# A selective scan on one core: eight turned states instead of seven, and delta's bias inside TensorE's product

## Chip, cores, metric

One core of a Trainium2 chip runs the whole program. The metric is the device time in microseconds (us) of one execution.

## What is computed

Two layers over eight images of 192 channels and 48 x 48 points: a selective state space layer and an attention layer. The scan of the first layer carries the time, and the change lies in it:

```python
dts = einsum('bkrl,kdr->bkdl', dts, dt_w)              # 12 rows -> 384 channels
delta = softplus(dts + dt_b[None, :, :, None])
A = -exp(A_logs)                                       # K = 4 directions, 384 channels, 16 states
def step(h, xs_t):
    d_t, u_t, B_t, C_t = xs_t
    h = h * exp(d_t[..., None] * A) + (d_t * u_t)[..., None] * B_t[:, :, None, :]
    y = einsum('bkdn,bkn->bkd', h, C_t)                # sum over the 16 states of C times h
    return (h, y)
```

All of it is float32. softplus(x) is computed as max(x, 0) + ln(1 + exp(-|x|)).

## The kernel before

The eight images are a loop (`Fori`). Each has a `front` (depthwise convolution, gelu, the projection to B, C and delta's 12 rows), a `scan_phase`, a `back` (layer norm, gate, output projection) and `attention`. The scan phase goes through K = 4 directions k of NC = 6 chunks each, so 24 **chunks** of CH = 384 positions an image, and 192 in all. Directions 1 and 3 run over the image by columns, so that their y is read and written with strides.

In each chunk a loop goes over the 16 **states** i, and in each state over J = 3 tiles j of 128 channels. The engines share one state after the other, each with an instruction order of its own that is written out by hand and never changes at run time; semaphores hold them together. Below, **slot i** is the part of an engine's loop with that i.

- ScalarE (ACT), slot i: three exponentials E(i, j) = exp(delta x A) into PSUM banks 2 to 4 (L1406). E(i, j) may start once VectorE has finished scan(i-1, j), which reads the same bank. Between and behind these three stand the other jobs: turned products P (L1365), `hold_state` (L1341), copies of a row of C into PSUM bank 1 (`c_copy`, L1357), the steps of softplus for the next chunk (x L1294, abs L1297, exp L1300, ln L1309), the stores of the last chunk's y (L1389, in slots 2 and 3) and the copies of two projection tiles (`unit_out`, only for k < 3).
- VectorE (DVE), slot i: three scans (L1098), one for each j. Scan(i, j) needs E(i, j).
- The product with C and the sum over the states have three ways. POOL_N: GpSimd multiplies (L1634), TensorE adds with a product by the identity (`state_sum`, L698). DVE_N: VectorE multiplies one slot later (`times_c`, L1120; needs the copied row), TensorE adds the same way. TURN_N: TensorE turns a 128 x 128 block so that positions lie on partitions (`turn`, T, L676, bank 0), ScalarE multiplies by C's column while it copies (P), and TensorE turns it back into the sum (`turned_sum`, S, L685). A state has three such blocks, numbered through the chunk: T(n), P(n), S(n) with n = 0 to 20. There is one bank for turned blocks, so T(n) waits for P(n-1) and P(n) for T(n): the two engines take turns.
- TensorE (PE), slot m: `slot` issues the turns, turned sums and state sums of tables TURN_AT and SUM_AT. Ahead of them come `delta_tile` (L664, delta's product for the next chunk into bank 1, in slots 1, 4, 7) and `unit` (L724, the projection tiles, bank 1, in slots 10 and 14), and behind them an addition of the previous y (L747, L750).
- GpSimd (POOL): delta x u x B of each state (L1624), at most three states ahead of the scans, the three C products (L1634), and delta x u once a chunk (L1613).

Bank 1 is shared in time by the C rows, delta's product and the projection tiles. ScalarE's and TensorE's queues are in order: what waits holds up all that stands behind it.

## Time and profile before

| | |
|---|---|
| median of 3 runs | 14456.84 us (14454.49 to 14457.94) |
| the profiled execution | 14456.79 us, its span 14455.0 us |
| scan phases in it | 8, each 24 chunks; the first from 161.58 us to about 1438 us |
| busy share of the span (page) | VectorE 87%, TensorE 84%, ScalarE 83%, GpSimd 69% |

A row of the timeline gives start, duration, engine, line, operation, and in brackets how long the engine was idle before it and who ended the wait. Durations of neighbours on one engine overlap a little, so the text goes from start to start.

### The profile page before, as it was taken

How to read it: one execution, taken by the hardware profiler on the slowest of the kernel's cores; microseconds unless marked ns; L12 is line 12 of the kernel's file. 1: busy time of each engine (PE TensorE's matmuls, PEld its weight loads, DVE VectorE, ACT ScalarE, POOL GpSimd, SP SyncE). 2: the span in 40 equal slices, each digit the busy share in tenths (PEclk: the TensorE clock that was granted, in tenths of full speed). 3: DMA queues.
4: the chain of work that ended last, by engine and by line, in shares of the span. 5: the costliest groups of instructions: out<-in, count | busy, mean ns of one | idle time of the engine just before them, and what ended most of it. 6: DMA issues, size and time to landing. Idle time of an engine off the chain costs nothing.

```text
span 14455.0 us, 270626 instructions
## 1 busy us (share of the span) xinstructions
PE 12184.4 (84%) x71128; PEld 7313.9 (51%) x71128; DVE 12643.8 (87%) x13653; ACT 11957.6 (83%) x25498; POOL 10046.1 (69%) x4006
## 2 busy tenths in 40 slices
PE   6887988879888798888988879888898888988889
PEld 4554554545555455554555545555455554555545
DVE  8999679997799977999689996899959999599995
ACT  5888788887888878887888878888788886888868
POOL 5999069990699807998079970899708996099960
PEclk9999999999999999999999999999999999999999
DMA  3443124440344303443034430344204442044420
GB/s 115 133 132 123 29 94 131 132 126 22 99 132 132 120 22 107 133 141 102 22 114 130 141 97 22 119 132 142 89 22 126 132 139 84 22 133 130 140 79 27
DMA packets 908103, 1470.10 MB, mean 102 GB/s; under 512 B 38913, under 2 KB 891905, under 8 KB 893665
## 3 DMA queue, kind: packets, MB, share of 16 engines
q1 hardware_dynamic: 906560, 1452.37, 31.5%
q8 instruction: 623, 10.21, 0.3%
q14 instruction: 920, 7.53, 0.2%
HBM read 1350.07 MB, written 102.17 MB: 100 GB/s over the span
## 4 chain that ended last, share of the span: by engine, by line
issue 39%; POOL 22%; PE 22%; DVE 10%; ACT 5%; DVEq 1%; ACTq 1%; POOLq 0%; DMA 0%; SPq 0%
POOL area L1624 18%; DVE area L1098 7%; PE ps L934 4%; PE ps L915 4%; PE ps L698 3%; POOL area L1613 2%; POOL area L1634 2%; PE ps L804 1%; ACT ps L1406 1%; DVE area L1120 1%; PE ps L676 1%; PE ps L780 1%; ACT area L1365 1%; DVE area L356 1%; PE ps L685 1%
## 5 line engine op out<-in xcount | busy, mean ns | idle before, releaser
L1098 DVE TENSOR_TENSOR_SCAN area<-ps,hst,area 128x384 f32<-128x384 f32 x9216 | 8566.2, 995 | 59.6 <-ACT ps L1406 46.9
L1624 POOL TENSOR_TENSOR area<-area 128x1152 f32<-128x1152 f32 x3072 | 7993.9, 2637 | 45.6 <-POOL area L1613 45.6
L1406 ACT ACTIVATE ps<-area,a_neg 128x384 f32<-128x384 f32 x9216 | 5171.5, 580 | 820.1 <-DVE area L1098 801.5
L698 PE MATMUL ps<-area,ident 128*128 128x384 f32 x10368 | 3845.6, 503 | 375.0 <-POOL area L1634 185.3
L676 PE MATMUL ps<-ident,area 128*128 128x128 f32 x12096 | 2117.6, 284 | 1353.7 <-ACT area L1365 1348.8
L698 PEld LDWEIGHTS ps<-area,ident 128*128 128x128 f32 x10368 | 1878.7, 195 | 1835.0 <-ACT area L1389 414.8
L676 PEld LDWEIGHTS ps<-ident,area 128*128 128x128 f32 x12096 | 1391.3, 141 | 2619.8 <-ACT area L1365 2019.7
L1365 ACT ACTIVATE area<-ps,area 128x384 f32<-128x384 f32 x4032 | 2304.7, 572 | 462.1 <-PE ps L676 438.6
L1567 ACT ACTIVATE area<-ps,t_neg,area 128x384 f32<-128x384 f32 x3456 | 2126.1, 667 | 113.6 <-PE ps L915 24.5
L1608 POOL TENSOR_TENSOR area<-area,ones 128x2304 f32<-128x2304 f32 x8 | 43.5, 5443 | 3060.6 <-ACT area L1321 2939.0
L685 PE MATMUL ps<-ident,area 128*128 128x128 f32 x12096 | 2017.1, 276 | 134.0 <-ACT area L1365 133.7
L1634 POOL TENSOR_TENSOR area<-area 128x1152 f32<-128x1152 f32 x576 | 1515.6, 2631 | 191.1 <-ACT hst L1341 190.5
L685 PEld LDWEIGHTS ps<-ident,area 128*128 128x128 f32 x12096 | 1459.8, 142 | 300.6 <-ACT area L1365 195.2
L1120 DVE TENSOR_TENSOR area<-area,ps 128x1152 f32<-128x1152 f32 x1152 | 1532.9, 1331 | 35.7 <-ACT ps L1357 35.7
L934 PE MATMUL ps<-area 64*64 64x384 f32 x13824 | 1479.5, 486 | 40.8 <-ACT area L1515 32.6
L915 PE MATMUL ps<-area 64*64 64x384 f32 x13824 | 1486.9, 489 | 12.7 <-ACT area L1491 12.7
L934 PEld LDWEIGHTS ps<-area 64*64 64x64 f32 x13824 | 614.1, 134 | 572.8 <-issue 159.1
L915 PEld LDWEIGHTS ps<-area 64*64 64x64 f32 x13824 | 627.2, 135 | 514.6 <-issue 85.1
L1188 DVE TENSOR_TENSOR area<-area 128x1920 f32<-128x1920 f32 (+1 forms) x32 | 43.4, 1356 | 874.0 <-ACT area L1515 874.0
L356 DVE SCALAR_TENSOR_TENSOR area<-area,w_dw 128x1152 f32<-128x1152 f32 (+1 forms) x640 | 802.8, 1331 | 0.0
L1357 ACT ACTIVATE ps<-area 128x384 f32<-128x384 f32 x1152 | 562.5, 488 | 24.2 <-DVE area L1120 8.3
L1613 POOL TENSOR_TENSOR area<-area 128x1152 f32<-128x1152 f32 x192 | 505.6, 2634 | 109.5 <-DVE area L1045 109.5
(140 smaller groups left out, 10052.8 us busy)
## 6 DMA issues: line engine op xcount, KB each, us to landing
area<-bc_rows SPq DMA_DIRECT2D x1536, 768.0 KB, 6.7
xz<-x_normed SPq DMA_DIRECT2D x144, 288.0 KB, 3.5
area<-in_x SPq DMA_DIRECT2D x18, 1728.0 KB, 10.0
area<-x_padded SPq DMA_DIRECT2D x24, 1250.0 KB, 5.6
z_raw<-z_st SPq DMA_DIRECT2D x144, 192.0 KB, 2.6
area<-z_raw SPq DMA_DIRECT2D x8, 3456.0 KB, 12.3
x_padded<-x_st SPq DMA_DIRECT2D x120, 200.0 KB, 7.3
x_normed<-area SPq DMA_DIRECT2D x9, 1728.0 KB, 7.9
```

Source lines behind the costliest of these rows:

```text
L676: i = e.matmul(ps[:, 0, j * 128:(j + 1) * 128], hb[:, n % NH, j, tt * 128:(tt + 1) * 128], ident[:], is_transpose=True)
L685: i = e.matmul(ps[:, 5 + j, tt * 128:(tt + 1) * 128], ht[:, tt, j * 128:(j + 1) * 128], ident[:], start=False, stop=False, is_transpose=True)
L698: m = e.matmul(ps[:, 5 + j, 0:CH], ident[:], hb[:, i % NH, j], start=i == 0, stop=i == N - 1)
L915: i = e.matmul(ps[64 * g:64 * g + 64, (2 * n + h) % 6, 0:CH], kz[64 * h:64 * h + 64, p, m * 128 + 64 * g:m * 128 + 64 * g + 64], q_v[64 * ...
L934: i = e.matmul(ps[64 * h:64 * h + 64, 6 + r, 0:CH], vt[64 * r:64 * r + 64, p, m, 64 * h:64 * h + 64], pb[64 * r:64 * r + 64, (2 * n + h) % ...
L1098: e.tensor_tensor_scan(rev(hb[:, i % NH, j], k), rev(ps[:, 2 + j, 0:CH], k), rev(dbu[:, i % NH, j], k), hst[:, i, j:j + 1], ALU.mult, ALU. ...
L1120: e.tensor_tensor(hb[:, i % NH], hb[:, i % NH], ps[:, 1:2, 0:CH].broadcast_to([128, J, CH]), ALU.mult).then_inc(hcs, 1)
L1365: e.activation(ht[:, tt], ps[:, 0, 0:CH], ACT.Copy, scale=c_t[:, ds(t + (k % 2 * MT + tt), 1), k // 2 * N + n]).then_inc(turn_cp, 1)
L1406: e.activation(ps[:, 2 + j, 0:CH], dlt[:, par, j], ACT.Exp, scale=a_neg[:, j, k, i:i + 1]).then_inc(da, 1)
L1567: e.activation(pb[:, w % 8], ps[:, w % 6, 0:CH], ACT.Exp, scale=ksc[:, p, 2 * m + h:2 * m + h + 1], bias=t_neg[:, 2 * p + h:2 * p + h + 1] ...
L1624: e.tensor_tensor(dbu[:, i % NH], du[:, par], row_b[:, q % 2, i % ROWS:i % ROWS + 1].broadcast_to([128, J, CH]), ALU.mult).then_inc(dbus, 1)
L1634: e.tensor_tensor(hb[:, i % NH], hb[:, i % NH], row_c[:, q % 2, i % ROWS:i % ROWS + 1].broadcast_to([128, J, CH]), ALU.mult).then_inc(hcp, 1)
```

## The change

One more state is turned (8 of 16), VectorE keeps five products (2, 5, 8, 12, 15), GpSimd its three. The blocks are n = 0 to 23, and the last two, 22 and 23, are done in slots 0 and 1 of the next chunk (TURN_AT[16]).

Delta's bias is a thirteenth row of `w_dt`, and the matching row of `dts` is one, so that TensorE adds it. The step x of softplus is gone: abs reads bank 1, ln writes into `du` instead of bank 1, and VectorE's delta step reads max(x, 0) from bank 1. The softplus steps start two slots earlier for each tile (abs in slots 1, 4, 7 at the slot's end, where it waits for `dp_mm`; exp and ln in the two slots after, behind E(i, 0)), and VectorE's delta step stands behind scan(i, 0) of slots 3, 6, 9. On TensorE `delta_tile` and `unit` move behind the slot's first turn and the previous turned sum (`between`).

```diff
-TURN_N = (1, 3, 6, 7, 10, 12, 13)
-TURN_AT = {2: (0,), 3: (1, 2), 4: (3, 4), 5: (5,), 7: (6, 7), 8: (8, 9), 9: (10, 11), 11: (12, 13), 12: (14,),
-           13: (15, 16), 14: (17, 18), 15: (19, 20)}
+TURN_N = (1, 3, 6, 7, 10, 11, 13, 14)
+TURN_AT = {2: (0,), 3: (1, 2), 4: (3, 4), 5: (5,), 7: (6, 7), 8: (8, 9), 9: (10, 11), 11: (12, 13), 12: (14, 15),
+           13: (16, 17), 14: (18, 19), 15: (20, 21), 16: (22, 23)}
-SUM_AT = {0: 3, 2: 4, 4: 6, 5: 7, 8: 10, 9: 12, 11: 13, 14: 16, 15: 17}
+SUM_AT = {0: 3, 2: 4, 4: 6, 5: 7, 8: 10, 9: 12, 12: 14, 15: 17}
-X_AT = {2: 0, 5: 1, 8: 2}
-SOFT = ((3, "abs", 0), (4, "exp", 0), (5, "ln", 0), (6, "abs", 1), (7, "exp", 1), (8, "ln", 1),
-        (9, "abs", 2), (10, "exp", 2), (11, "ln", 2))
+SOFT = ((1, "abs", 0), (2, "exp", 0), (3, "ln", 0), (4, "abs", 1), (5, "exp", 1), (6, "ln", 1),
+        (7, "abs", 2), (8, "exp", 2), (9, "ln", 2))
+STEP_AT = {3: 0, 6: 1, 9: 2}
@@ sync: after the loads of the constants
+            e.wait_ge(consts, 16 * len(loads))
+            for k in range(K):
+                e.dma_start(w_dt[DT0[k] + R:DT0[k] + R + 1, k].rearrange("o (j p) -> o j p", j=J),
+                            t["b_dt"][:, :, k:k + 1].rearrange("p j o -> o j p"),
+                            allow_slow_non_contiguous=True).then_inc(bias_row, 16)
@@ tensor
+            e.wait_ge(bias_row, 16 * K)
...
-                def slot(g, m):
+                def slot(g, m, between=None):
...
                         turned_sum(g, before[-1])
+                    if between:
+                        between()
...
-                        if m < 2 and last:
-                            slot(g - 1, N + m)
...
+                        if m < 2 and last:
+                            slot(g - 1, N + m, between)
+                            slot(g, m)
+                        else:
+                            slot(g, m, between)
@@ vector
-                e.scalar_tensor_tensor(out=dlt[:, par, j], in0=dlt[:, par, j], scalar=0.0, in1=ps[:, bank, 0:CH],
+                e.scalar_tensor_tensor(out=dlt[:, par, j], in0=ps[:, bank, 0:CH], scalar=0.0, in1=du[:, par, j],
...
+                            if nxt and j == 0 and i in STEP_AT:
+                                delta(g + 1, 1 - par, STEP_AT[i])
@@ scalar
-                if op == "x":
+                if op == "abs":
                     e.wait_ge(dp_mm, g * 3 + (j + 1))
-                    e.activation(x, ps[:, bank, 0:CH], ACT.Identity, bias=b_dt[:, j, k:k + 1]).then_inc(dp_rd, 1)
+                    e.activation(y, ps[:, bank, 0:CH], ACT.Abs).then_inc(dp_a, 1)
...
-                    e.activation(ps[:, bank, 0:CH], y, ACT.Ln, bias=1.0).then_inc(dp_a, 1)
+                    e.activation(y, y, ACT.Ln, bias=1.0).then_inc(dp_a, 1)
...
-                             ACT.Copy).then_inc(xp_ev, 1)
+                             ACT.Identity, bias=dt_one[64:128]).then_inc(xp_ev, 1)
...
-                    if nxt and i in (5, 8, 11):
-                        e.wait_ge(dp_v, g * 3 + (3 + (i - 2) // 3))
+                    if nxt and i in (2, 5, 8):
+                        e.wait_ge(dp_v, g * 3 + (3 + (i - 2) // 3 + 1))
...
+                            if nxt and j == 0:
+                                for at, op, d in SOFT:
+                                    if at == i and op != "abs" and (last or d):
+                                        softplus(g + 1, 1 - par, op, d)
...
-                            elif last:
-                                turned_products(g - 1, *last, N - 1, j)
+                            if i < 2 and last:
+                                turned_products(g - 1, *last, N - 1 + i, j)
```

**ScalarE, end of slot 4 and start of slot 5.** Before (L1365 is P(2), L1341 the hold, L1300 softplus's exp of tile 0, L1406 E(5, 0)):

```order
L1365 ACTIVATE area<-ps,area 128x384 [waits turn_sum]
L1341 ACTIVATE hst<-area 128x3
L1299 ISA
L1300 ACTIVATE area<-area 128x384 [waits dp_a]
L1405 REGISTER_ALU
L1406 ACTIVATE ps<-area,a_neg 128x384 [waits scan]
```

After (L1368 is P(2), L1308 the abs of tile 1, L1409 E(5, 0), L1311 softplus's exp of tile 1, then P(3)):

```order
L1368 ACTIVATE area<-ps,area 128x384 [waits turn_sum]
L1344 ACTIVATE hst<-area 128x3
L1307 REGISTER_ALU
L1308 ACTIVATE area<-ps 128x384 [waits dp_mm]
L1408 REGISTER_ALU
L1409 ACTIVATE ps<-area,a_neg 128x384 [waits scan]
L1310 REGISTER_ALU
L1311 ACTIVATE area<-area 128x384 [waits dp_a]
```

A step that read ScalarE's own result stood there; now one stands there that waits for TensorE's product of this same slot.

**ScalarE, slot 13.** Before: E(13, 0), E(13, 1), P(14), E(13, 2):

```order
L1406 ACTIVATE ps<-area,a_neg 128x384 [waits scan]
L1405 REGISTER_ALU
L1406 ACTIVATE ps<-area,a_neg 128x384 [waits scan]
L1363 REGISTER_ALU
L1365 ACTIVATE area<-ps,area 128x384 [waits turn_sum,turn_mm]
L1405 REGISTER_ALU
L1406 ACTIVATE ps<-area,a_neg 128x384 [waits scan]
```

After: E(13, 0), P(14), E(13, 1), E(13, 2), P(15):

```order
L1409 ACTIVATE ps<-area,a_neg 128x384 [waits scan]
L1366 REGISTER_ALU
L1368 ACTIVATE area<-ps,area 128x384 [waits turn_sum,turn_mm]
L1408 REGISTER_ALU
L1409 ACTIVATE ps<-area,a_neg 128x384 [waits scan]
L1408 REGISTER_ALU
L1409 ACTIVATE ps<-area,a_neg 128x384 [waits scan]
L1366 REGISTER_ALU
L1368 ACTIVATE area<-ps,area 128x384 [waits turn_sum,turn_mm]
```

P(14) has moved ahead of E(13, 1).

**TensorE, slot 14.** Before: the unit (L724), T(17), S(16), then T(18) and S(17):

```order
L724 MATMUL ps<-xz,w_in 128x384 [waits xz_in,hcs]
L724 MATMUL ps<-xz,w_in 128x384
L674 REGISTER_ALU
L676 MATMUL ps<-ident,area 128x128 [waits turn_cp]
L676 MATMUL ps<-ident,area 128x128 x2
L685 MATMUL ps<-ident,area 128x128 [waits turn_cp]
L685 MATMUL ps<-ident,area 128x128 x2
```

After: T(18) (L682), S(17) (L691), the unit (L732), the sum of state 12 (L704), T(19):

```order
L682 MATMUL ps<-ident,area 128x128 [waits turn_cp]
L682 MATMUL ps<-ident,area 128x128 x2
L691 MATMUL ps<-ident,area 128x128 [waits turn_cp]
L691 MATMUL ps<-ident,area 128x128 x2
L728 REGISTER_ALU
L732 MATMUL ps<-xz,w_in 128x384 [waits xz_in,hcs]
L732 MATMUL ps<-xz,w_in 128x384
L704 MATMUL ps<-area,ident 128x384 [waits hcs]
L704 MATMUL ps<-area,ident 128x384 x2
L680 REGISTER_ALU
L682 MATMUL ps<-ident,area 128x128 [waits turn_cp]
L682 MATMUL ps<-ident,area 128x128 x2
```

Both the unit and a state sum now stand between the two turns of the slot.

## Rows read from the trace of the kernel before

**Rows 1.** Busy time by window: length, PE, PEld, DVE, ACT, POOL, clock, DMA, GB/s.

```profile
905.00:1380.00 475.00, 378.45 (x1761) 232.81 (x1760) 473.91 (x513) 416.94 (x963) 467.24 (x181) 1.00 0.42 134
```

**Rows 2.** Groups by line: VectorE's scans; busy, mean ns, idle before and releasers.

```profile
L1098 DVE TENSOR_TENSOR_SCAN area<-ps,hst,area 128x384 f32<-128x384 f32 x9216 | 8566.2, 995 | 59.6 <-ACT ps L1406 46.9 <-POOL area L1624 5.5 <-PE ps L698 3.8
```

**Rows 3.** Timeline of VectorE: scans, one C product, delta step, scans.

```profile
1021.18 8.28 DVE L1098 TENSOR_TENSOR_SCAN area<-ps,hst,area 128x384 f32<-128x384 f32 x9
1029.38 1.33 DVE L1120 TENSOR_TENSOR area<-area,ps 128x1152 f32<-128x1152 f32 x1
1030.62 5.55 DVE L1098 TENSOR_TENSOR_SCAN area<-ps,hst,area 128x384 f32<-128x384 f32 x6
1036.09 0.53 DVE L1045 SCALAR_TENSOR_TENSOR area<-area,ps 128x384 f32<-128x384 f32 x1
1036.54 2.83 DVE L1098 TENSOR_TENSOR_SCAN area<-ps,hst,area 128x384 f32<-128x384 f32 x3
```

**Rows 4.** Timeline of GpSimd over one chunk.

```profile
1064.54 10.40 POOL L1624 TENSOR_TENSOR area<-area 128x1152 f32<-128x1152 f32 x4 [0.24 <-POOL area L1613]
1074.89 2.64 POOL L1634 TENSOR_TENSOR area<-area 128x1152 f32<-128x1152 f32 x1
1077.48 10.42 POOL L1624 TENSOR_TENSOR area<-area 128x1152 f32<-128x1152 f32 x4
...
1114.53 2.62 POOL L1613 TENSOR_TENSOR area<-area 128x1152 f32<-128x1152 f32 x1
1117.39 10.40 POOL L1624 TENSOR_TENSOR area<-area 128x1152 f32<-128x1152 f32 x4 [0.24 <-POOL area L1613]
```

**Rows 5.** One line, L1613 (once a chunk), first image: duration min/median/max, first and last start.

```profile
L1613 POOL TENSOR_TENSOR area<-area x24: 2615/2637/2674, 155.9 to 1378.6; 128x1152 f32<-128x1152 f32 x24
```

**Rows 6.** Timeline of ScalarE and TensorE, slots 11 to 13, direction 2.

```profile
1001.96 0.57 ACT L1406 ACTIVATE ps<-area,a_neg 128x384 f32<-128x384 f32 x1
1002.47 0.56 ACT L1365 ACTIVATE area<-ps,area 128x384 f32<-128x384 f32 x1
...
1003.08 0.55 PE L676 MATMUL ps<-ident,area 128*128 128x128 f32 x3 [1.16 <-ACT area L1365]
...
1003.46 0.49 PE L685 MATMUL ps<-ident,area 128*128 128x128 f32 x3
...
1004.44 2.10 PE L698 MATMUL ps<-area,ident 128*128 128x384 f32 x6
...
1006.37 0.49 PE L676 MATMUL ps<-ident,area 128*128 128x128 f32 x3
...
1006.90 0.58 ACT L1365 ACTIVATE area<-ps,area 128x384 f32<-128x384 f32 x1 [0.91 <-PE ps L676]
```

**Rows 7.** Timeline of all three, slots 12 to 15, direction 1.

```profile
628.29 0.56 ACT L1365 ACTIVATE area<-ps,area 128x384 f32<-128x384 f32 x1
...
633.37 0.58 ACT L1365 ACTIVATE area<-ps,area 128x384 f32<-128x384 f32 x1 [1.54 <-PE ps L676]
...
637.31 1.46 PE L724 MATMUL ps<-xz,w_in 96*128 96x384 f32 x4
...
638.60 0.49 PE L676 MATMUL ps<-ident,area 128*128 128x128 f32 x3
...
639.13 0.58 ACT L1365 ACTIVATE area<-ps,area 128x384 f32<-128x384 f32 x1 [0.80 <-PE ps L676]
639.61 1.08 ACT L1406 ACTIVATE ps<-area,a_neg 128x384 f32<-128x384 f32 x2
...
640.22 1.93 DVE L1098 TENSOR_TENSOR_SCAN area<-ps,hst,area 128x384 f32<-128x384 f32 x2 [0.49 <-ACT ps L1406]
```

**Rows 8.** Timeline: delta's product on TensorE and the step that reads it.

```profile
381.97 0.81 PE L664 MATMUL ps<-area,w_dt 128*128 128x384 f32 x2
...
382.82 0.58 ACT L1294 ACTIVATE area<-ps,b_dt 128x384 f32<-128x384 f32 x1 [0.38 <-PE ps L664]
```

**Rows 9.** One line, L1389, the stores of y: duration min/median/max.

```profile
L1389 ACT ACTIVATE area<-ps x576: 464/644/860, 225.6 to 13970.7; 128x384 f32<-128x384 f32 x192
```

More of the change, by code:

```diff
@@ L216, in build @@
         prepared = sem("prepared")
+        bias_row = sem("bias_row")
         exp_a = sem("exp_a")
@@ L731, in body, with between @@
                     for m in range(N):
-                        j = DELTA_AT.get(m) if nxt else None
-                        if j is not None:
-                            e.wait_ge(hcs, gd + (1, 2, 3)[j])
-                            delta_tile(*nxt, j, 1)
-                        if k < UK and m in UNIT_AT:
-                            unit(k, h, gd, UNIT_AT.index(m))
-                        if m < 2 and last:
-                            slot(g - 1, N + m)
+                        def between():
+                            j = DELTA_AT.get(m) if nxt else None
+                            if j is not None:
+                                e.wait_ge(hcs, gd + (1, 2, 3)[j])
+                                delta_tile(*nxt, j, 1)
+                            if k < UK and m in UNIT_AT:
+                                unit(k, h, gd, UNIT_AT.index(m))
                         if m == 3 and not last:
@@ L742, in body @@
                             e.wait_ge(ct_cp, b * GM + GM)
-                        slot(g, m)
+                        if m < 2 and last:
[3 more added lines that the diff above has]
+                            slot(g, m, between)
                         if m in ADD_AT:
@@ L1108, in body @@
                             times_c(g, i - 1)
-                        if nxt and i in LN_AT:
-                            delta(g + 1, 1 - par, LN_AT[i])
                 def times_c(g, i):
@@ L1287, in _, with softplus @@
             group_std(1, 0)
-            def softplus(g, par, k, op, j, bank=1, h=None):
-                x, y = dlt[:, par, j], du[:, par, j]
-                if op == "x":
+            def softplus(g, par, op, j, bank=1):
+                y = du[:, par, j]
+                if op == "abs":
                     e.wait_ge(dp_mm, g * 3 + (j + 1))
-                    e.activation(x, ps[:, bank, 0:CH], ACT.Identity, bias=b_dt[:, j, k:k + 1]).then_inc(dp_rd, 1)
-                elif op == "abs":
-                    e.wait_ge(dp_rd, g * 3 + (j + 1))
-                    e.activation(y, x, ACT.Abs).then_inc(dp_a, 1)
+                    e.activation(y, ps[:, bank, 0:CH], ACT.Abs).then_inc(dp_a, 1)
                 elif op == "exp":
@@ L1327, in front @@
                 dt_rows(b, 0, 1)
-                for j in range(J):
-                    softplus(g0, 0, 0, "x", j, 5 + j)
                 for n, (_, op, j) in enumerate(SOFT):
@@ L1332, in front @@
                         dt_rows(b, 0, 2 + n // 2)
-                    softplus(g0, 0, 0, op, j, 5 + j)
+                    softplus(g0, 0, op, j, 5 + j)
                 dt_rows(b, 1, 0)
@@ L1401, in body @@
                     for i in range(N):
-                        if nxt and i == 3:
+                        if nxt and i == 1:
                             e.wait_ge(dbus, g16 + 8)
@@ L1426, in body @@
                             unit_out(h, UNIT_AT.index(i - 1))
-                        if nxt and i in LN_AT:
-                            softplus(g + 1, 1 - par, nxt[0], "ln", LN_AT[i], h=h if i == 11 else None)
                         if i >= 1:
@@ L1436, in body @@
                         if nxt:
-                            for at, op, j in SOFT:
-                                if at == i and op != "ln":
-                                    softplus(g + 1, 1 - par, nxt[0], op, j)
+                            for at, op, d in SOFT:
+                                if i == 2 and d == 0 and not last or at == i and op == "abs" and (last or d):
+                                    softplus(g + 1, 1 - par, op, d)
                 walk(e, body)
@@ L1445, in scan_phase @@
                 c_copy(g, N - 1, None)
-                for at in turns(N - 1):
+                for at in turns(N - 1) + turns(N):
                     turned_product(g, K - 1, NC - 1, at)
```

34 lines of the change are left out of this document (13 added, 21 removed).

## Prediction

> **What bounds the kernel now.** I read the busy time by window first, inside a scan phase. In 475 us VectorE is busy 473.9, GpSimd 467.2, ScalarE 416.9 and TensorE 378.5 [rows 1]. VectorE sets the pace, and GpSimd stands 1.4% behind it. The group of the scans says the same: 9216 scans, 59.6 us idle before all of them together [rows 2]. The clock is at its full level there.
>
> The timelines of the two give their bare work in one chunk. VectorE: nine scans take 8.20 from start to start (1021.18 to 1029.38), 0.912 each; a C product 1.24; a delta step 0.45 [rows 3]. So 48 x 0.912 + 6 x 1.24 + 3 x 0.45 = 52.56. GpSimd: four products 10.35 (2.588 each), a C product 2.59, the once-a-chunk product 2.86 with its wait [rows 4]. So 16 x 2.588 + 3 x 2.59 + 2.86 = 52.04. The chunk really takes 52.85 (1064.54 to 1117.39), VectorE's work and 0.3 of waits. Over the first image the mean is (1378.6 - 155.9) / 23 = 53.16 [rows 5]; direction 1 is slower than the others, which rows 7 explain below.
>
> **What the change removes.** VectorE loses one C product: bare work 52.56 - 1.24 = 51.32. GpSimd's 52.04 stays. If those two were all, the period would fall to 52.04. ScalarE gives up three x steps and one C copy and gets three turned products, each about 0.46 from start to start (the row at 639.13, then 639.61) [rows 7]: total about 0.4 less. So no engine is overloaded in the sum. TensorE loses a state sum of 1.93 (1004.44 to 1006.37) and gets three turns and three turned sums of 0.38 or less [rows 6]: no change.
>
> **What it does to the order.** ScalarE and TensorE are in order and hand one bank back and forth, so I followed that chain from slot to slot, with distances from start to start: P to the next T 0.61; T to S 0.38; state sum 1.93 [rows 6]; unit 1.29 (637.31 to 638.60); T to P 0.53; E to E 0.50; start of E to the scan that it feeds 0.61 (639.61 to 640.22) [rows 7]; delta's product to its reader 0.85 [rows 8]. E(i+1, j) cannot start before scan(i, j) has ended, 1.03 behind its start (995 ns [rows 2] and a few hundredths). For the short steps I take hold 0.10, store 0.37, copy 0.42, softplus steps 0.45, the durations less their overlap. That this works I tested on the slowest place of before, direction 1. With the unit at 637.31, T(17) comes 1.29 later, P(17) 0.53 behind it at 639.13, E(15, 1) at 639.61, and scan(15, 1) at 640.22, with 0.49 of idle [rows 7]. So one late P holds VectorE up even where ScalarE has slack on average. That is also why that direction is slow.
>
> **Term A, slots 0 to 5: abs waits for TensorE.** Abs of tile 0 stands at the end of slot 1. Delta's product needs VectorE's last C product and stands behind S(23), which needs P(23): P(23) to abs is 0.61 + 0.38 (S) + 0.85 = 1.8, of which 0.56 are P and hold: ScalarE idles 1.25. Abs of tile 1, end of slot 4: P(2) to T(3) 0.61, S(2) 0.38, delta's product 0.35, abs 0.85, so 2.2 less 0.56: 1.6 idle. Both stand ahead of exponentials. Take all that ScalarE does from E(0, 0) to E(5, 1): 16 exponentials 8.2, eight P 3.7, five softplus steps 2.2, three stores 1.1, two copies 0.8, five holds 0.5, the last exponential 0.6, the two waits 2.85: 20.0. E(0, 0) starts 0.6 before scan(0, 0), so scan(5, 1) starts at 19.4. VectorE's bare work up to there is 17 scans, two C products, one delta step, less a little: 17.5. **A = 1.9 a chunk**. Lower end: if ScalarE reaches slot 3 without lateness, E(3, 0) starts 1.71 before scan(3, 0), 10.3 of work and wait follow, bare VectorE needs 8.1: 0.5. The long store is 0.35 to 0.4 longer than the short one [rows 9], 0.25 of it from start to start: in direction 1 A is 0.75 more (2.6); in direction 3, which has no units and arrives that much earlier, 1.9 again.
>
> **Term B, slot 13.** P(14) now stands ahead of E(13, 1). From P(12) to P(14) the trace has 1002.47 to 1006.90 = 4.43 (T(13), S(12), an addition, the sum of state 9, T(14)) [rows 6]; with strides 628.29 to 633.37 = 5.08 [rows 7]. P(12) starts 1.55 to 1.8 after scan(11, 0) (1.03, an exponential; with a unit's copy a bit later). P(14) to scan(13, 1) is 0.46 + 0.61. Sum 7.3; bare VectorE, seven scans, 6.4. **B = 0.9**, with strides 1.6, direction 3 1.3. Lower end 0.65 (P(12) at its earliest). Before, E(13, 1) stood ahead of that P, and slot 12 had a C product that covered it.
>
> **Term C, slots 14 and 15, directions 0 to 2.** P(17) comes 4.4 behind P(14) (six exponentials' and products' worth of work and a copy). Then T(18) 0.61, S(17) 0.38, unit 0.35 + 1.29, state sum 1.93, T to P 0.53: P(19) 5.1 behind P(17). Behind it hold, the unit's copy and E(0, 0): 1.6 to scan(0, 0). From scan(13, 1): 4.4 + 5.1 + 1.6 - 1.1 = 10.0; bare VectorE there, eight scans and a C product, 8.5. **C = 1.5**. Direction 3 has no units: 0.
>
> Once VectorE is later than GpSimd's 52.04, GpSimd only runs ahead, and is no bound.
>
> **Sum.** Chunk times: directions 0 and 2, 51.3 + 1.9 + 0.9 + 1.5 = 55.6; direction 1, 51.3 + 2.6 + 1.6 + 1.5 = 57.0; direction 3, 51.3 + 1.9 + 1.3 = 54.5. Mean 55.7 against 53.1 to 53.2 [rows 5]: +2.6 x 192 = +500. The first and the last chunk of an image have less of A: -2 an image, -16. The two turns left at an image's end cost 2, three x steps of the front give 1.5 back: nothing. The four bias transfers are issued at about 13 us behind the constants, and TensorE starts near 28 us: cover of 15, at most 10 if it failed. Total +480 on the profiled 14456.8 (span 14455.0, median 14456.84: the same): **14,935 us**.
>
> **Low and high.** With all lower ends, 51.3 + 0.5 + 0.65 + 1.5 = 53.95 in directions 0 and 2, 55.3 in 1 and 53.9 in 3: mean 54.3, +1.15 x 192 = +220, 14,680. Upwards, 1 us a chunk for abs of tile 2 or a sum that waits for GpSimd in slots 3 and 6: 15,120.
>
> **Rivals.** (1) Faster: the waits are absorbed, since ScalarE idles 12% in the window [rows 1], and only bare work counts. Then GpSimd binds at 52.04: 24 x 52.04 = 1249 an image against 24 x 53.16 = 1276, -27 x 8 = -216: 14,250. For: VectorE is full. Against: 640.22 [rows 7] shows that average slack doesn't absorb. It decides for A, B, C together under 0.7 a chunk. The Trainium skill (Perfetto Trace Analysis, Identifying the Most-Contended Engine) tells one to optimize the engine of the highest occupancy first; by that rule, with nothing behind it, the 1.24 would come back whole, 192 x 1.24 = 238, 14,219, which is this rival and not my sum. Chance 0.14.
> (2) Half: A is hidden, because TensorE's product comes in while ScalarE has other work; B and C stay: 53.4 in directions 0 and 2, 54.2 and 52.6: mean 53.4, +0.25 x 192 = +50, 14,510; with part of A up to 14,680. For: in before the product is there before its reader in most chunks. Against: it is now behind S of the same slot. Chance 0.16.
> (3) Worse: further places, above 15,120. Chance 0.08.
> (4) The forecast, 14,680 to 15,120: 0.62.
>
> **Numbers.** About 0.2% (29 us) is what a measurement of this kernel tells from no change. Faster has rival 1: 0.15; a mix of 1 and 2 falls within: 0.05; slower 0.80. The range takes the forecast and rival 2, 14,480 to 15,120.
>
> **What would show it.** Idle time before VectorE's scans of 59.6 [rows 2] should rise to some 800 us, released by ScalarE's exponentials, at scans (5, 0), (5, 1), (13, 1) and (0, 0) of a chunk; ScalarE should wait for TensorE's delta product for some 2 to 3 us a chunk (abs), and for P(14) and P(19) about 1.5 each; L1613 should be 54.3 to 57 apart. I am wrong if VectorE stays at 99% in the window, or if abs finds its product ready.

## The result and the profile after

The changed kernel takes 14980.4 us (median of 4, 14976.7 to 14989.0) against 14457.4 us of the kernel before (4 runs): 1.0362 times as long, interval 1.0344 to 1.038. It is slower by 523 us. The forecast was 14,935 us, in a range of 14,480 to 15,120, with 0.80 on slower. The profiled execution has a span of 14975.5 us.

The first view is the groups of instructions by line: engine, operation, count, then busy us and mean ns, then the idle time just before them and what ended it. L1112 are the scans (L1098 before), L1368 the turned products, L1637 GpSimd's products with C.

```profile
L1112 DVE TENSOR_TENSOR_SCAN area<-ps,hst,area 128x384 f32<-128x384 f32 x9216 | 8673.4, 1001 | 729.8 <-ACT ps L1409 552.0 <-PE ps L704 171.2 <-POOL area L1627 6.4
...
L1368 ACT ACTIVATE area<-ps,area 128x384 f32<-128x384 f32 x4608 | 2653.9, 576 | 791.5 <-PE ps L682 777.0
...
L1637 POOL TENSOR_TENSOR area<-area 128x1152 f32<-128x1152 f32 x576 | 1515.1, 2630 | 688.5 <-ACT hst L1344 497.7 <-DVE area L1112 181.9
...
L1134 DVE TENSOR_TENSOR area<-area,ps 128x1152 f32<-128x1152 f32 x960 | 1277.0, 1330 | 5.9 <-ACT ps L1360 5.9
```

The idle time before the scans went from 59.6 [rows 2] to 729.8 us. The prediction said some 800. Of it 552.0 us end with an exponential of ScalarE, as forecast, and 171.2 with a state sum of TensorE, which the prediction did not name. The scans' own busy time grew by 107 us too, from 8566.2 to 8673.4: in a run of scans one follows the next after 0.912 us [rows 3], since their tails overlap; a scan before a wait lasts its full 1.02 and nothing overlaps its end. So each wait costs about 0.1 us beyond its printed idle time. Against these 777 us (670 of idle time and 107) stand 256 us that the C products lost: 192 of them are gone, 1277.0 us are left, and in the kernel before the same view has 1532.9:

```profile
L1120 DVE TENSOR_TENSOR area<-area,ps 128x1152 f32<-128x1152 f32 x1152 | 1532.9, 1331 | 35.7 <-ACT ps L1357 35.7
```

The difference, 521 us, is the 523 us that the change costs. GpSimd got slack: 688.5 us of idle time stand before its C products, which wait for holds and scans.

The window of rows 1 again: span, then busy time of TensorE, its weight load, VectorE, ScalarE and GpSimd, with the clock.

```profile
905.00:1380.00 475.00, 366.61 (x1784) 229.66 (x1782) 447.52 (x483) 393.87 (x915) 445.28 (x172) 1.00 0.40 129
```

VectorE falls from 473.91 [rows 1] to 447.52 of 475, GpSimd from 467.24 to 445.28. All engines are less busy than before, the granted clock is 1.00 in both windows, and the kernel is slower: no engine is overloaded, they wait for each other.

The absolute values (L1308, three a chunk) with the wait before them, in us and the number of times, and GpSimd's once-a-chunk product of the first image:

```profile
L1308 ACT ACTIVATE area<-ps x576: 491/491/496, 143.7 to 14399.9; 128x384 f32<-128x384 f32 x192
...
  PE ps L670: 765.4, 544
```

```profile
L1616 POOL TENSOR_TENSOR area<-area x24: 2623/2640/2666, 154.4 to 1441.6; 128x1152 f32<-128x1152 f32 x24
```

ScalarE waits 765.4 us for delta's product, 4.0 us a chunk; the forecast had 2 to 3. In the chunk of the timeline below the three absolute values wait 1.19, 1.51 and 1.50 us; the sum of term A had the first two (1.25 and 1.6), and behind the third, in slot 7, no scan waits. (1441.6 - 154.4) / 23 = 55.97 is the mean chunk of the first image, against 53.16 [rows 5]: 2.81 more, and 192 x 2.81 = 540, near the 523 measured.

VectorE's timeline in one chunk of direction 2, the rows with a wait (start, duration, then the instructions merged in the row, in brackets the idle time before them and its end):

```profile
1008.01 2.90 DVE L1112 TENSOR_TENSOR_SCAN area<-ps,hst,area 128x384 f32<-128x384 f32 x3 [1.38 <-ACT ps L1409]
...
1015.20 3.75 DVE L1112 TENSOR_TENSOR_SCAN area<-ps,hst,area 128x384 f32<-128x384 f32 x4 [0.30 <-ACT ps L1409]
...
1025.82 1.02 DVE L1112 TENSOR_TENSOR_SCAN area<-ps,hst,area 128x384 f32<-128x384 f32 x1 [0.57 <-ACT ps L1409]
1027.20 2.84 DVE L1112 TENSOR_TENSOR_SCAN area<-ps,hst,area 128x384 f32<-128x384 f32 x3 [0.37 <-ACT ps L1409]
...
1052.27 1.02 DVE L1112 TENSOR_TENSOR_SCAN area<-ps,hst,area 128x384 f32<-128x384 f32 x1 [0.61 <-PE ps L704]
1053.60 1.93 DVE L1112 TENSOR_TENSOR_SCAN area<-ps,hst,area 128x384 f32<-128x384 f32 x2 [0.31 <-ACT ps L1409]
```

These are scans (0,0), (2,0), (5,0), (5,1), (13,0) and (13,1). The first is term C, the next three are A, the last two B. No other scan of the chunk waits over 0.12 us. The sum of the six is 3.54 and, with 0.1 for each tail, 4.1; 51.3 of bare work and 4.1 are 55.4, and the chunk takes 55.6.

The mechanism of A, at slot 4's end. TensorE's S(2) and delta's product (L670), then ScalarE's abs and E(5,0):

```profile
1023.64 0.49 PE L691 MATMUL ps<-ident,area 128*128 128x128 f32 x3
1023.97 0.81 PE L670 MATMUL ps<-area,w_dt 128*128 128x384 f32 x2
```

```profile
1024.81 0.49 ACT L1308 ACTIVATE area<-ps 128x384 f32<-128x384 f32 x1 [1.51 <-PE ps L670]
1025.20 0.58 ACT L1409 ACTIVATE ps<-area,a_neg 128x384 f32<-128x384 f32 x1
```

B, slot 13: TensorE's addition (L762), the sum of state 9 (L704), T(14) (L682), and ScalarE's P(14):

```profile
1049.40 0.81 PE L762 MATMUL ps<-area,ident 128*128 128x384 f32 x2
1050.05 2.10 PE L704 MATMUL ps<-area,ident 128*128 128x384 f32 x6
1051.98 0.49 PE L682 MATMUL ps<-ident,area 128*128 128x128 f32 x3
```

```profile
1052.51 0.58 ACT L1368 ACTIVATE area<-ps,area 128x384 f32<-128x384 f32 x1 [1.83 <-PE ps L682]
```

C, slot 14: unit (L732), state sum, T(19), and ScalarE's P(17) and P(19):

```profile
1002.68 1.46 PE L732 MATMUL ps<-xz,w_in 96*128 96x384 f32 x4
1003.98 2.10 PE L704 MATMUL ps<-area,ident 128*128 128x384 f32 x6
1005.91 0.49 PE L682 MATMUL ps<-ident,area 128*128 128x128 f32 x3
```

```profile
1001.35 0.57 ACT L1368 ACTIVATE area<-ps,area 128x384 f32<-128x384 f32 x1
...
1006.44 0.58 ACT L1368 ACTIVATE area<-ps,area 128x384 f32<-128x384 f32 x1 [1.92 <-PE ps L682]
```

In B and C, ScalarE idles 1.83 and 1.92 us (the forecast had about 1.5 each) for a turn that TensorE does behind a state sum, and the exponential behind that P comes late.

Last, a chunk of direction 1 (strided), the rows where it differs, scans (3,2), (5,0) and (13,0):

```profile
623.46 1.02 DVE L1112 TENSOR_TENSOR_SCAN area<-ps,hst,area 128x384 f32<-128x384 f32 x1 [0.56 <-ACT ps L1409]
...
629.74 1.02 DVE L1112 TENSOR_TENSOR_SCAN area<-ps,hst,area 128x384 f32<-128x384 f32 x1 [1.27 <-ACT ps L1409]
...
657.04 1.02 DVE L1112 TENSOR_TENSOR_SCAN area<-ps,hst,area 128x384 f32<-128x384 f32 x1 [1.46 <-PE ps L704]
```

The second is not the same in all chunks of direction 1: scan (5,0) waits 0.56 us in some (they take 57.1 us) and 1.27 in others (57.8).

### The profile page after: what moved, and what is told of

It reads as the page before. It is cut to its first block, busy times and chain, and to the rows that moved or that the text cites. A ratio compares the mean times of both kernels' runs of the same rounds, so it can differ in the third digit from the quotient of the medians.

```text
span 14975.5 us, 275415 instructions
## 1 busy us (share of the span) xinstructions
PE 12266.8 (82%) x73432; PEld 7420.9 (50%) x73432; DVE 12505.4 (84%) x13462; ACT 11861.5 (79%) x25306; POOL 10049.7 (67%) x4006
## 4 chain that ended last, share of the span: by engine, by line
PE 34%; issue 28%; ACT 15%; POOL 15%; DVE 6%; ACTq 1%; DMA 0%; DVEq 0%; POOLq 0%; SPq 0%
POOL area L1627 11%; PE ps L704 9%; ACT ps L1409 6%; ACT area L1368 5%; PE ps L946 4%; PE ps L927 4%; PE ps L682 4%; POOL area L1637 4%; DVE area L1112 3%; PE ps L732 2%; PE ps L691 2%; PE ps L762 1%; PE ps L792 1%; PE ps L816 1%; ACT ps L1360 1%
## 5 line engine op out<-in xcount | busy, mean ns | idle before, releaser
L1112 DVE TENSOR_TENSOR_SCAN area<-ps,hst,area 128x384 f32<-128x384 f32 x9216 | 8673.4, 1001 | 729.8 <-ACT ps L1409 552.0
L1409 ACT ACTIVATE ps<-area,a_neg 128x384 f32<-128x384 f32 x9216 | 5199.6, 583 | 383.5 <-DVE area L1112 351.7
L682 PE MATMUL ps<-ident,area 128*128 128x128 f32 x13824 | 2460.0, 287 | 1687.2 <-ACT area L1368 1673.2
L704 PE MATMUL ps<-area,ident 128*128 128x384 f32 x9216 | 3389.4, 498 | 465.5 <-ACT area L1392 262.6
L1368 ACT ACTIVATE area<-ps,area 128x384 f32<-128x384 f32 x4608 | 2653.9, 576 | 791.5 <-PE ps L682 777.0
L682 PEld LDWEIGHTS ps<-ident,area 128*128 128x128 f32 x13824 | 1532.2, 141 | 3063.2 <-ACT area L1368 2727.8
L704 PEld LDWEIGHTS ps<-area,ident 128*128 128x128 f32 x9216 | 1690.3, 191 | 1968.9 <-ACT area L1392 531.7
L691 PE MATMUL ps<-ident,area 128*128 128x128 f32 x13824 | 2290.9, 275 | 230.4 <-ACT area L1368 230.4
L1570 ACT ACTIVATE area<-ps,t_neg,area 128x384 f32<-128x384 f32 x3456 | 2128.8, 668 | 142.5 <-PE ps L927 56.6
L1637 POOL TENSOR_TENSOR area<-area 128x1152 f32<-128x1152 f32 x576 | 1515.1, 2630 | 688.5 <-ACT hst L1344 497.7
L691 PEld LDWEIGHTS ps<-ident,area 128*128 128x128 f32 x13824 | 1648.3, 141 | 381.7 <-ACT area L1368 321.4
L1134 DVE TENSOR_TENSOR area<-area,ps 128x1152 f32<-128x1152 f32 x960 | 1277.0, 1330 | 5.9 <-ACT ps L1360 5.9
L1308 ACT ACTIVATE area<-ps 128x384 f32<-128x384 f32 x576 | 282.9, 491 | 766.2 <-PE ps L670 765.4
```

The lines of the kernel that those rows point to most:

```text
L682: i = e.matmul(ps[:, 0, j * 128:(j + 1) * 128], hb[:, n % NH, j, tt * 128:(tt + 1) * 128], ident[:], is_transpose=True)
L691: i = e.matmul(ps[:, 5 + j, tt * 128:(tt + 1) * 128], ht[:, tt, j * 128:(j + 1) * 128], ident[:], start=False, stop=False, is_transpose=True)
L704: m = e.matmul(ps[:, 5 + j, 0:CH], ident[:], hb[:, i % NH, j], start=i == 0, stop=i == N - 1)
L1112: e.tensor_tensor_scan(rev(hb[:, i % NH, j], k), rev(ps[:, 2 + j, 0:CH], k), rev(dbu[:, i % NH, j], k), hst[:, i, j:j + 1], ALU.mult, ALU. ...
L1134: e.tensor_tensor(hb[:, i % NH], hb[:, i % NH], ps[:, 1:2, 0:CH].broadcast_to([128, J, CH]), ALU.mult).then_inc(hcs, 1)
L1368: e.activation(ht[:, tt], ps[:, 0, 0:CH], ACT.Copy, scale=c_t[:, ds(t + (k % 2 * MT + tt), 1), k // 2 * N + n]).then_inc(turn_cp, 1)
```

## Experiments

The theory: the time lies in three places of the hand-written order (A, B, C), not in the amount of work. The rivals: the eighth state's work is itself too much, or a wait that is removed turns up elsewhere. The runs of the kernel before beside these had medians of 14,454 to 14,459 us. A time without a range or an interval is one execution.

### The two halves of the change

The bias half alone, with the tables of before for the turned states:

```
-TURN_N = (1, 3, 6, 7, 10, 11, 13, 14)
+TURN_N = (1, 3, 6, 7, 10, 12, 13)
-... 11: (12, 13), 12: (14, 15), 13: (16, 17), 14: (18, 19), 15: (20, 21), 16: (22, 23)}
+... 11: (12, 13), 12: (14,), 13: (15, 16), 14: (17, 18), 15: (19, 20)}
-SUM_AT = {0: 3, 2: 4, 4: 6, 5: 7, 8: 10, 9: 12, 12: 14, 15: 17}
+SUM_AT = {0: 3, 2: 4, 4: 6, 5: 7, 8: 10, 9: 12, 11: 13, 14: 16, 15: 17}
```

> The change without its eighth turned state: seven states turned, in the places they had before, and the rest of the change kept (the bias as a row of ones in TensorE's product, x read in PSUM, the split of the C products as the tables of before give it). Theory (order): term A is owned by this half, since the absolute value still stands between the delta product and E(i,0), so about 1.6 us a chunk over 192 chunks come back as a wait, while VectorE's and GpSimd's work of before stays; the time is 14,500 to 14,750 us, ScalarE's absolute values wait about 4 us a chunk for TensorE, and there is no wait of scan (0,0) of 1.4 us. Rival (the eighth state alone costs): the time stays within 50 us of the kernel before, 14,410 to 14,510 us.

14637.8 us, +183 on the kernel before, as the theory had it. Its absolute values wait 847.8 us for TensorE, but the scans wait only 185.9 us. So the bias half costs by itself, and part of A does not reach the scans as long as VectorE has six C products: in a chunk of direction 2 that takes 53.4 us, scan (5,1) alone waits, 0.37 us.

The turning half alone: the same tables put into the kernel before, with its softplus.

> The kernel before with eight states turned and five C products on VectorE, in the places of the change, and its own softplus and bias kept (ScalarE's identity with the bias, x in SBUF). Theory (order): this half owns the waits of slots 13 to 15 (terms B and C) and not term A, so VectorE waits 1.1 us at scans (13,0) and (13,1) and 1.4 us at scan (0,0), and the time is 14,620 to 14,740 us, about 1.56 us x 192 = 300 us below the whole change and still slower than before. Rival (turning pays by itself, and it is the bias half that costs): the period of a chunk goes to GpSimd's 52.04 us and the time is 14,200 to 14,350 us.

14508.0 us, +49: a miss, over 100 us below the theory's range and far above the rival's. Its waits in one chunk of direction 2, the scans (13,0), (13,1) and (0,0):

```profile
1008.49 1.02 DVE L1098 TENSOR_TENSOR_SCAN area<-ps,hst,area 128x384 f32<-128x384 f32 x1 [0.38 <-PE ps L698]
1009.82 1.93 DVE L1098 TENSOR_TENSOR_SCAN area<-ps,hst,area 128x384 f32<-128x384 f32 x2 [0.31 <-ACT ps L1406]
1019.13 2.90 DVE L1098 TENSOR_TENSOR_SCAN area<-ps,hst,area 128x384 f32<-128x384 f32 x3 [0.67 <-ACT ps L1406]
```

No wait of slots 2 to 5 is there, so A is the bias half's. But C is 0.67, not 1.38. The reason stands in TensorE's rows of slot 14: the unit (L724) is ahead of T(18), as in the kernel before, not between T(18) and T(19).

```profile
1013.05 1.56 PE L724 MATMUL ps<-xz,w_in 96*128 96x384 f32 x4
1014.44 0.49 PE L676 MATMUL ps<-ident,area 128*128 128x128 f32 x3
1014.77 0.49 PE L685 MATMUL ps<-ident,area 128*128 128x128 f32 x3
1015.10 2.10 PE L698 MATMUL ps<-area,ident 128*128 128x384 f32 x6
```

ScalarE's P(17) and P(19) there:

```profile
1013.18 0.57 ACT L1365 ACTIVATE area<-ps,area 128x384 f32<-128x384 f32 x1
...
1017.56 0.58 ACT L1365 ACTIVATE area<-ps,area 128x384 f32<-128x384 f32 x1 [1.03 <-PE ps L676]
```

P(17) to P(19) is 4.38 us here and 5.09 in the change, 0.71 more, and scan (0,0) waits 0.67 here and 1.38 there, 0.71 more as well. So half of C goes with the unit's place behind the turn, which came with the bias half. The halves cost 183 and 49, together 232; the whole costs 523. The rest, 291 us, exists only when both are in. The traces place it. Added up over the run without the first chunk of each image, the scans' idle time of A (slots 2 to 6) is 273 us in the whole change, 139 in the bias half and 3 in the turning half; of B (slot 13) 221, 17 and 178; of C (slot 0) 199, 0 and 96. So 131 us of idle time at A, 26 at B and 103 at C come only with both, 260 in all, and most of the remaining 31 are the tails of the further waits at A. With a C product less VectorE is early enough to meet all of A, and C doubles when the unit stands between the two turns.

### A: the absolute values one place later

```
-SOFT = ((1, "abs", 0), (2, "exp", 0), (3, "ln", 0), (4, "abs", 1), ...
+SOFT = ((2, "abs", 0), (2, "exp", 0), (3, "ln", 0), (5, "abs", 1), ...
+SOFT_J = {"abs": 1, "exp": 2, "ln": 0}
-    if at == i and op != "abs" and (last or d):
+    if at == i and j == SOFT_J[op] and (last or d):
```

> The change with one edit: the absolute values of the next chunk's delta stand one place later, behind E(2,1), E(5,1) and E(8,1), and their exponentials behind the second E of the same slot, so that a delta product has an exponential more to finish behind. Theory (order, term A): the waits of VectorE for exponentials at scans (2,0), (5,0) and (5,1), together 1.56 us a chunk, go; 192 chunks x 1.56 us = 300 us, the time is 14,650 to 14,760 us. Rival (ScalarE's rate, not the order, sets these waits): the absolute values are as many and as long, so the wait only moves to scans (2,1), (5,1) or (8,0), and the time stays within 60 us of 14,980 us.

14766.8 us, 214 less than the change; the theory had 300 and a range that ended 7 us lower, so it misses by a little. The scans' group:

```profile
L1113 DVE TENSOR_TENSOR_SCAN area<-ps,hst,area 128x384 f32<-128x384 f32 x9216 | 8622.3, 995 | 561.2 <-ACT ps L1410 367.8 <-PE ps L705 186.9 <-POOL area L1628 6.3
```

552.0 us released by ScalarE became 367.8. In directions 0 and 2 the waits of slots 2 to 5 are gone, one of 0.26 us stands at scan (6,0), and B and C stand as before. Over the run 93 us of A's 273 stay, at scan (6,0) and, next to strided stores, at scan (3,2). The rival that ScalarE's rate sets A falls: it does the same work in another order, and the chunk goes from 55.6 to 54.3 there, from 57.1 to 57.8 down to 55.8 in direction 1.

The same edit on the bias half alone:

> The bias half alone (seven states turned as before), with the absolute values one place later, behind the second exponential of slots 2, 5 and 8. Theory (term A is all that the bias half costs): VectorE's waits in slots 2 to 5 go and the time falls from 14,638 us to 14,400 to 14,490 us, within 50 us of the kernel before. Rival (the row of ones and x in PSUM cost beyond the place of the absolute value, by VectorE's step reading PSUM or the bank being held longer): the time stays above 14,560 us.

14532.9 us: between the two. 105 of the 183 us that this half cost came back; some 75 stay, above the 14,490 that the theory allowed and below the rival's 14,560. Directions 0 and 2 are at 53.0, against 52.9 before. What stays is in direction 1 (54.6 against 53.8 a chunk), where a C product waits 1.07 us for its row's copy behind the unit, and in direction 3 (53.7 against 52.8 on average), where scan (3,2) waits 0.38 us and scan (6,0) 0.28 to 1.13. So the place of the absolute values is most of what the bias half costs, not all.

### B: slot 13

```
-ADD_AT = {5: 0, 8: 1, 11: 2}
+ADD_AT = {5: 0, 8: 1, 12: 2}
-                    if len(now) == 2 and j != 1:
-                        turned_product(g, k, c, now[j // 2])
+                    if len(now) == 2 and (j != 1 if m != 12 else j != 0):
+                        turned_product(g, k, c, now[j // 2 if m != 12 else j - 1])
```

> The change with slot 13 arranged otherwise: the turned products P(14) and P(15) stand behind E(13,1) and E(13,2) instead of behind E(13,0) and E(13,2), and TensorE's third addition of a chunk stands a slot later. Theory (term B): VectorE's waits at scans (13,0) and (13,1), together 0.9 to 1.1 us a chunk, go; the time is 14,770 to 14,850 us. The part that scan (13,0) waits for TensorE's sum of state 9, 0.6 us, goes only because the addition no longer stands ahead of that sum; if it stays, the gain is 0.3 to 0.5 us a chunk, 14,880 to 14,920 us. Rival (VectorE waits there because it is early, whatever the order): the wait turns up at the next scan and the time stays within 60 us of 14,980 us.

14790.4 us, 190 less, within the theory's range. The scans' group:

```profile
L1112 DVE TENSOR_TENSOR_SCAN area<-ps,hst,area 128x384 f32<-128x384 f32 x9216 | 8645.7, 996 | 569.0 <-ACT ps L1409 547.0 <-POOL area L1627 6.2 <-PE ps L704 5.5
```

The 171.2 us behind TensorE's sums are gone (5.5), and so are the waits at (13,1): ScalarE's total hardly moves, since scan (0,0) now waits 1.54 instead of 1.38 us, 2.00 in direction 1, and slots 2 to 5 wait as before. So part of the removed wait turned up at scan (0,0), in direction 1 above all, which is a small part of the rival. A chunk takes 54.6 to 54.7 in directions 0 and 2. B was real, net 0.95 us a chunk there and 0.9 to 1.2 in directions 1 and 3.

### C: three attempts on slot 14

First, the unit behind the whole slot 14, and ScalarE's copy of it in the next chunk's slot 0, ahead of the copy of C's row 15:

```
+                        elif m == UNIT_AT[1]:
+                            slot(g, m)
+                            between()
                         else:
                             slot(g, m, between)
```

> The change with slot 14's unit of the output projection placed behind the whole slot, not between T(18) and T(19), and its gate of z moved to the start of the next chunk. Theory (term C): in directions 0 and 2, where scan (0,0) of a chunk waits 1.4 us, the wait goes; half to three quarters of the 192 chunks x 1.4 us = 140 to 200 us, the time is 14,780 to 14,850 us. Rival (the unit's time is owed in any place, since TensorE's and ScalarE's chain through slots 14 and 15 is as long): scan (0,0) goes on waiting over 1 us, or scan (0,1) does, and the time stays within 60 us of 14,980 us.

15056.8 us, 76 more than the change. Scan (0,0) no longer waits, but (0,1) waits 0.65 us, the C product behind it 0.24, and (2,0) 0.54 in some chunks and 1.2 to 1.5 in others. In directions 0 and 2 the first kind takes 55.4 us, a little less than the change's 55.6, and the second 56.6; why a chunk is of one kind or the other was not followed. That is the rival, if 76 us is a little over the 60 that it named: behind T(19) the unit is ahead of T(20), and the same bank is late one turn further.

Second, both units where no turned product competes, slots 6 and 10:

```
-UNIT_AT = (10, 14)
+UNIT_AT = (6, 10)
                                 e.wait_ge(hcs, gd + (1, 2, 3)[j])
+                                if k < UK and j == 2:
+                                    e.wait_ge(unit_ev, h * 2 + 1)
```

> The change with the two units of the output projection's input in slots 6 and 10, in place of 10 and 14: slot 6 has no turned product and slot 14 has two. Theory (term C is TensorE's 1.46 us unit standing in the ping-pong of turned products): scan (0,0) waits 0.3 us or less instead of 1.4 us in 144 chunks, the time is 14,760 to 14,850 us. Rival (as the run with the unit behind slot 14 suggests, two turned products a slot with a step of 1.48 us each are themselves too slow for slots 13 to 15, unit or not): scan (0,0) still waits 0.7 us or more and the time is 14,880 us or more.

15102.8 us, 122 more. Scan (0,0) is free, as the theory said, but the time went the other way: it lies in the rival's range, and the rival's cause, a wait at scan (0,0), is not there. Bank 1 is the unit's and delta's; ScalarE's, TensorE's and VectorE's rows at the end of slot 7, down to scan (8,0):

```profile
1045.73 0.49 ACT L1384 ACTIVATE x_st<-ps 128x384 f32<-128x384 f32 x1 [2.31 <-PE ps L732]
```

```profile
1046.28 0.91 PE L670 MATMUL ps<-area,w_dt 128*128 128x384 f32 x2 [0.33 <-ACT x_st L1384]
```

```profile
1048.23 1.02 DVE L1114 TENSOR_TENSOR_SCAN area<-ps,hst,area 128x384 f32<-128x384 f32 x1 [1.57 <-ACT ps L1409]
```

The unit waits for VectorE's product with the row of state 5, its copy waits for the unit (2.31 us of idle ScalarE), delta's product waits for the copy, and abs for that. This run says nothing against C; it shows what one more user of bank 1 costs in those slots.

Third, one turned product fewer in slot 14:

```
-           13: (16, 17), 14: (18, 19), 15: (20, 21), 16: (22, 23)}
+           13: (16, 17), 14: (18,), 15: (19, 20), 16: (21, 22), 17: (23,)}
-SUM_AT = {..., 12: 14, 15: 17}
+SUM_AT = {..., 12: 14, 15: 18}
```

> The change with one turned product fewer in slot 14, where the second unit stands: P(18) alone there, P(19) and P(20) in slot 15, P(21) and P(22) in the next chunk's slot 0, P(23) in its slot 1, and the last state sum a slot later. Theory (term C is two turned products and a unit meeting in one slot): scan (0,0) waits 0.4 us or less instead of 1.4 us in 144 chunks, the time is 14,760 to 14,860 us. Rival (the chain of turned products of slots 11 to 16 is late as a whole, at 1.48 us a step): the wait moves to scans (0,1) to (2,0) or to the stores of slots 2 and 3, and the time stays at 14,920 us or more.

15432.3 us, 452 more, which is what the rival said: scan (0,0) is free, but (2,0) waits 0.62 us, and ScalarE's store of y (L1393), which needs the last turned sum and the last state sum, now waits for both, and VectorE behind it:

```profile
1044.76 0.49 ACT L1309 ACTIVATE area<-ps 128x384 f32<-128x384 f32 x1 [1.52 <-PE ps L670]
...
1049.71 0.49 ACT L1393 ACTIVATE area<-ps 128x384 f32<-128x384 f32 x1 [1.97 <-PE ps L704]
```

```profile
1050.71 1.02 DVE L1113 TENSOR_TENSOR_SCAN area<-ps,hst,area 128x384 f32<-128x384 f32 x1 [2.05 <-ACT ps L1410]
```

This is scan (3,0); in other chunks it waits 3.49 us or more. The edit moves two things one slot later, P(23) and the sum of state 15. P(23) stands behind A's wait for delta's product, the sum behind S(23), and the store behind that sum. Which of the two moves costs more was not run apart. Both lie on the way to the store, so the chain has no free place at the chunk's end.

### Mended versions

All three places at once, C by slots 6 and 10:

> The change with all three places mended: absolute values one place later, P(14) and P(15) behind E(13,1) and E(13,2) with the third addition a slot later, units in slots 6 and 10. Theory (waits by order, not work): VectorE's 51.3 us of work a chunk lie below GpSimd's 52.04 us, so a chunk takes 52.1 to 52.9 us and the time is 14,250 to 14,420 us, faster than both kernels. Rival (the eighth state's work on TensorE and ScalarE bounds a chunk whatever the order): over 54 us a chunk, 14,560 us or more.

14609.7 us, 1.0106 [1.0089, 1.0122] of before. With C by the thinner slot 14 instead:

> The change with its absolute values one place later, P(14) and P(15) behind E(13,1) and E(13,2), and one turned product fewer in slot 14 (terms A, B and C mended, the units left in slots 10 and 14). Theory (waits by order, not work): a chunk of directions 0 and 2 takes 52.1 to 52.9 us, one of direction 1 some 54 us, and the time is 14,290 to 14,430 us, below both kernels. Rival (a new wait stands where each was removed): 53.5 us or more in directions 0 and 2, 14,550 us or more.

14704.0 us, 1.0171 [1.0154, 1.0188]. They are 371 and 276 us faster than the change, slower than before, and outside what the theory said. The time of the first lies in its rival's range, though its chunks of directions 0 and 2, at 53.7 us, are under the 54 that the rival named. The second meets its rival in both numbers (53.9 us a chunk, over 14,550 us): a new wait stands where one was removed. The gains of A and B are there, and the mended C brings a wait of 1.04 us at scan (9,0) in the first and of 1.44 us at scan (3,0) in the second.

The turning half with B's edit and the thinner slot 14:

> The turning half alone (the softplus and bias of the kernel before) with P(14) and P(15) behind E(13,1) and E(13,2), the third addition a slot later and one turned product fewer in slot 14. Theory: the waits left in the turning half alone, 0.7 us at scans (13,0) and (13,1) and 0.7 us at scan (0,0), go, VectorE's work of 51.4 us falls below GpSimd's 52.04 us, a chunk takes 52.1 to 52.6 us and the time is 14,270 to 14,380 us. Rival (ScalarE, which keeps the identity with the bias and the eighth state's 1.7 us a chunk, is the next bound): a chunk stays at 53.0 us or more and the time at 14,450 us or more.

14540.8 us, 1.0057 [1.004, 1.0074]; a miss. The numbers fit the rival (53.1 us a chunk, over 14,450 us) but not its cause: the waits in slots 13 to 0 are gone, and one of 1.12 us stands at scan (3,0), behind the store of y, which waits 1.98 us for the sum of state 15. The absolute values of this kernel read ScalarE's own result and not delta's product, so that wait comes without A too. So the thinner slot is what costs here, and the last run leaves it out: the turning half with B's edit and nothing else.

> The turning half alone (the softplus and bias of the kernel before, its unit ahead of the slot's turned product) with P(14) and P(15) behind E(13,1) and E(13,2) and the third addition a slot later; the turned products of slots 14 to 16 stay where the change has them, so no store of y waits for a late one. Theory (the waits at scans (13,0) and (13,1), 0.7 us and about 0.2 us more, are the last that lie above GpSimd's 52.04 us): the 53.1 us of directions 0 and 2 become 52.2 to 52.4 us, direction 1 gains 1.1 us and direction 3 0.5 us, and the time is 14,508 - 154 = 14,354 us, between 14,310 and 14,400 us, below both kernels. Rival (each wait removed there returns at scan (0,0), as slots 14 and 15 become later): within 40 us of 14,508 us.

14336.3 us (14326.4 to 14340.0), 0.9917 [0.9901, 0.9934] of before, and 644 us below the change. The theory holds, within its 14,310 to 14,400. The gain over the kernel before is small, but its interval ends below 1. The scans' group, the window of rows 1, and GpSimd's timeline:

```profile
L1098 DVE TENSOR_TENSOR_SCAN area<-ps,hst,area 128x384 f32<-128x384 f32 x9216 | 8574.7, 993 | 168.6 <-ACT ps L1406 157.1 <-POOL area L1624 5.5
```

```profile
905.00:1380.00 475.00, 379.24 (x1878) 243.85 (x1877) 469.17 (x510) 430.39 (x988) 471.08 (x182) 0.99 0.42 134
```

```profile
994.88 2.64 POOL L1613 TENSOR_TENSOR area<-area 128x1152 f32<-128x1152 f32 x1
997.76 10.41 POOL L1624 TENSOR_TENSOR area<-area 128x1152 f32<-128x1152 f32 x4 [0.24 <-POOL area L1613]
...
1047.05 2.63 POOL L1613 TENSOR_TENSOR area<-area 128x1152 f32<-128x1152 f32 x1
```

GpSimd is now the busiest engine (471.08 of 475), its once-a-chunk product comes every 1047.05 - 994.88 = 52.17 us, and nothing in this chunk waits on it but the usual 0.24. That is, within 0.2 us, the bound of 52.04 that the prediction's first rival named: the kernel comes to it in directions 0 and 2 and in most chunks of direction 3; direction 1 stays at 52.8. Scan (0,0) still waits 0.67 us in directions 0 and 2, as in the turning half alone, and 1.02 instead of 0.67 in direction 1: part of what was removed at slot 13 came back there. The eighth turned state is a gain of 0.8% in this order; with the change's softplus no order that was run is faster than the kernel before.

## Why the prediction was right, point by point

**Bounds.** VectorE with GpSimd right behind it: right. The mended turning half comes down to 52.15 us in directions 0 and 2, next to GpSimd's 52.04 of bare work.

**What the change removes.** 1.24 us a chunk were given for the C product; measured 192 products of 1.33 us busy, 256 us in all. That is 1.33 with the overlapped ends and 1.24 without: right. "No engine is overloaded in the sum" is borne out too: the runs with the change's work in another order went from 14,610 to 15,432 us.

**Term A**, forecast 1.9 us in directions 0 and 2, measured 0.30 + 0.57 + 0.37 and 0.1 of tail each, 1.5. The mechanism is right link by link: P(2) at 1022.61 to the absolute value at 1024.81 is 2.20, forecast 2.2. The term that was mis-sized is the sum: from scan (0,0) to scan (5,1) it had 19.4 us, and the trace has 1027.20 - 1008.01 = 19.19. The two waits in it are 0.06 and 0.09 shorter than forecast, and against its own 17.5 of bare work A would be 1.7. Direction 1 was forecast at 2.6 and has 2.2 in some chunks and 2.9 in others, with a wait of 0.56 at scan (3,2) that the sum had as hidden, and direction 3 has 2.2 for 1.9. Mending it gave 1.3 a chunk back in directions 0 and 2, since a wait of 0.26 stays.

**Term B**, forecast 0.9, 1.6 in direction 1 and 1.3 in direction 3; measured 1.1, 1.97 and 1.36. The size is near, but the step missed a wait: scan (13,0) needs the buffer of `hb` that state 9 leaves, and TensorE's sum of state 9 stands behind the same addition (171.2 us over the run). The prediction followed the P's only and took buffers as free.

**Term C**, forecast 1.5, measured 1.38 of idle and 0.1 of tail. Right, with its conditions (absent inside direction 3, which has no units) and link by link: P(17) to P(19) was forecast at 5.1 and is 1006.44 - 1001.35 = 5.09. The turning half added what the sum does not tell, that the unit's place between the turns is half of C.

**The sum.** Chunks of directions 0 and 2, of 1 and of 3 were forecast at 55.6, 57.0 and 54.5 us and took 55.6, 57.1 to 57.8, and 55.0: the first right by errors that cancel (A up to 0.4 too large, B 0.2 too small, and a rest of 0.2), so that its exactness is luck; the others short by up to 0.8 and by 0.5. The step to the total took 2.6 a chunk; against the measured mean of 53.16 it is 2.5, some 15 us less. 14,935 was 45 us too low.

**The rivals.** The first (14,250, GpSimd binds) lost, since waits of 4.1 us a chunk are far over its 0.7. Its bound is where the mended turning half ends, at 14,336, still 86 us above its number, with direction 1 at 52.8. The Trainium skill's advice to optimize the engine of the highest occupancy first (Perfetto Trace Analysis, Identifying the Most-Contended Engine) pointed at VectorE; that work was taken from it and the kernel got slower, by 3.6%. The second rival (A hidden, 14,510) has by chance the time of the turning half, 14,508, where there is no A. Its own sum is too low: B and C whole give 51.3 + 0.9 + 1.5 = 53.7 and 54.4, not 53.4 and 54.2, and so some 14,540.

**What stays open.** A and B mended together, with C left alone, was not run; if the two gains add, that is an estimate of 14,980 - 214 - 190 = 14,576 us, below both mended versions of the whole and above the kernel before. The 291 us of interplay are placed by idle time and not tested one by one. C itself was never removed without a new wait, so that its price of 1.5 us a chunk rests on the timeline and on the smaller value of the turning half, not on a run without it. B's edit moves two things at once, the addition and the two P's, and which of them frees which scan was not tried.
